# Eight experts over tokens sorted by their expert through DRAM, in place of every expert over every token

## The chip, the cores and the metric

The kernel is one program on one core of a Trainium2 chip (trn2). The metric is device time in microseconds (us), from the start of the execution to its end. A profiled execution also gives the span between its first and last recorded instruction, which is a little shorter. Engines are PE (matmuls), DVE (vector), ACT (scalar, activations), POOL (GpSimd) and SP (which here issues DMAs).

## What is computed

A network of eight stages over x, 4 batches of 512 tokens with 128 features (2048 tokens, 16 tiles of 128 rows). Each stage adds `tanh(gate) * f(layernorm(x))` to x. The stages are: a 16-head attention, **eight experts with one expert per token**, a one-head attention, a small attention with experts, a masked attention, a ternary feed-forward, a decoder block, and a mixture of 16 experts. The change is in the second stage, and reaches into the first:

```
gate_logits = einsum('bsd,ed->bse', x, gate_w) + gate_b + expert_bias
top_idx = argmax(gate_logits, axis=-1)
for e in range(8):
    mask = (top_idx == e)[..., None]
    h = relu(einsum('bsd,df->bsf', x, w1[e]) + b1[e])     # 128 -> 512
    y = einsum('bsf,fd->bsd', h, w2[e]) + b2[e]           # 512 -> 128
    out = out + mask * y
```

## The kernel before

The code is written per engine: for each stage there is one function for PE, ACT, DVE (`_ve`), POOL (`_po`) and SP, and each engine runs its functions in program order. They meet only at semaphores: `mark` names an event, `at` waits for it. Nothing reorders the instructions later. `x` stays in SBUF, token rows on partitions; `xn` is its layernorm, and `xt` is `xn` transposed (features on partitions), made by `follow_measure` (DVE, L379 to L384), `follow_power` (POOL, L389), `follow_scale` (DVE, L395), `follow_turn` (PE, L424) and `follow_turned` (ACT, L430). A batch's x of the next stage is measured as soon as it is final.

Matmuls that must be exact to fp32 are made from bf16 halves: a value is its high part plus a low part, and `products` (L449) issues three matmuls (high x high, high x low, low x high). `split_po` splits the experts' weights w1 and w2 on POOL during the first stage, so that `split_view` gives for each block of 512 columns the high and the low part.

**First stage** (`image_*`): 256 steps, one per batch, head and query tile. In a step PE makes 128x666 scores (L638), DVE takes the maximum (L692), ACT the exponential (L790), PE transposes (L649), ACT and DVE copy (L805, L710), POOL subtracts the high part to get the low part (L903), and PE multiplies with the values (L665). `image_chores(i)` says which extra work a step carries. Every eight steps SP issues two DMAs that copy keys between partition halves (`work<-work`). The last four pieces of the stage are PE's output products L593, each followed by DVE's addition to x (L739).

**Experts' stage** (`experts_*`): 32 rounds, for each batch b of 512 tokens and each expert e. `up` issues 4 x 3 matmuls of 512 columns (weights stationary, `xt1` moving) into banks 0 to 4. ACT evicts every bank twice with relu, once rounded to bf16 as the high part (L1021) and once whole (L1024), DVE subtracts them to the low part (L1043). `down` issues for 4 token tiles and 4 parts of the hidden width 3 matmuls of 128 columns, hidden activations stationary and w2 moving, so its result has token rows on partitions. DVE adds it to x with the weight `hot * gate` (L1052), which is 0 for tokens of other experts. All tokens thus go through all experts. PE's order is up(0), up(1), then the turn of batch 3, the router (L476), the one-hot and the biases b2 (L483, L989), then up(k), down(k-1) for all k. The next stage's x of batches 0 to 2 is measured, scaled and turned between the rounds. The stage begins when the last x of the first stage is added (`barrier(…, 1)`) and ends with the last L1052. `experts_sp` loads the weights of four later stages at its start.

## Time and profile before

| | us |
|---|---|
| median of 3 runs | 2153.85 |
| lowest and highest run | 2153.39, 2156.68 |
| the profiled execution's own time | 2150.68 |
| its span | 2148.9 |
| PE, DVE, ACT, POOL busy in the span | 1728.8, 1321.8, 966.7, 599.1 |
| granted PE clock, mean over the span | 0.895 |

The profile is of one execution. Its page groups busy time by engine and line, and follows back the chain of work that ended last. A granted clock of 1.00 stands for TensorE's 2.4 GHz, 0.50 for 1.2 GHz. Busy time of PE is of pipelined matmuls with modelled ends, so durations of many in a row are read from starts.

### The profile page before, as it was taken

What the parts mean: (1) busy time and instruction counts of PE and PEld (TensorE: products, weight loads), DVE (VectorE), ACT (ScalarE), POOL (GpSimd) and SP (SyncE); (2) the same over time, 40 slices, a digit from 0 to 9 for tenths busy, and PEclk for the clock granted to TensorE, in tenths of its full rate; (3) what the DMA queues carried; (4) which work ended last, traced back from release to release, by engine and by line L of the source; (5) the groups of instructions that cost most, each with busy time, mean ns of one, the idle gap of its engine ahead of it and who ended that gap; (6) DMA issues with size and microseconds to landing.
All of it is one profiled execution on the core that took longest, in us unless ns stands there. A gap on an engine that the chain in (4) does not pass through costs nothing.

```text
span 2148.9 us, 34188 instructions
## 1 busy us (share of the span) xinstructions
PE 1728.8 (80%) x12709; PEld 1075.3 (50%) x12848; DVE 1321.8 (62%) x3131; ACT 966.7 (45%) x2073; POOL 599.1 (28%) x723
## 2 busy tenths in 40 slices
PE   4899889988988987999623978996985886579997
PEld 2566656665666655776413644552444333424444
DVE  6777677767767744776487575655457455643333
ACT  4677557756766744997100633553321443201111
POOL 3567567656545540000000224200001200200000
PEclk9999989998999997999665788998997787789998
DMA  5000000000000001001000000000000000000000
GB/s 206 14 14 21 14 14 14 20 14 14 14 14 17 17 9 72 2 2 69 6 0 0 1 8 5 1 2 1 1 1 1 1 1 1 0 0 0 6 5 10
DMA packets 14598, 33.01 MB, mean 15 GB/s; under 512 B 3594, under 2 KB 9058, under 8 KB 13538
## 3 DMA queue, kind: packets, MB, share of 16 engines
q1 hardware_dynamic: 14433, 30.81, 4.6%
q8 instruction: 104, 1.70, 0.3%
q14 instruction: 61, 0.49, 0.1%
HBM read 18.84 MB, written 1.05 MB: 9 GB/s over the span
## 4 chain that ended last, share of the span: by engine, by line
PE 56%; DVE 27%; issue 7%; ACT 7%; POOL 2%; DMA 0%; ACTq 0%; DVEq 0%; POOLq 0%
PE banks L449 14%; DVE work L692 4%; PE banks L649 4%; PE banks L665 3%; PE banks L2288 3%; PE banks L1672 3%; PE banks L638 3%; PE banks L2284 3%; DVE xn L395 2%; DVE work L710 2%; ACT work L790 2%; PE banks L593 2%; PE banks L1655 1%; PE banks L424 1%; PE banks L2336 1%
## 5 line engine op out<-in xcount | busy, mean ns | idle before, releaser
L903 POOL TENSOR_TENSOR work<-work 128x512 bf16<-128x512 f32 (+1 forms) x448 | 374.1, 862 | 79.5 <-ACT work L805 75.7
L790 ACT ACTIVATE work<-banks,work 128x666 f32<-128x666 f32 x256 | 208.5, 814 | 251.3 <-DVE work L692 172.3
L649 PE MATMUL banks<-const,work 128*128 128x128 f32 (+1 forms) x1536 | 234.8, 285 | 51.1 <-ACT work L805 45.2
L389 POOL TENSOR_TENSOR norm_room<-norm_room,minus_half 128x4 f32<-128x4 f32 x48 | 50.0, 1041 | 757.1 <-DVE norm_room L384 757.1
L692 DVE TENSOR_REDUCE work<-banks 128x1 f32<-128x666 f32 x256 | 215.8, 843 | 63.7 <-PE banks L638 63.1
L649 PEld LDWEIGHTS banks<-const,work 128*128 128x128 f32 (+1 forms) x1536 | 158.3, 136 | 101.9 <-ACT work L790 53.2
L449 PE MATMUL banks<-work,weights_b 128*128 128x512 bf16 x823 | 192.6, 389 | 16.2 <-DVE work L1996 5.6
L665 PE MATMUL banks<-work 128*64 128x256 bf16 (+1 forms) x2304 | 177.7, 283 | 11.6 <-POOL work L903 10.5
L638 PE MATMUL banks<-work 128*128 128x154 bf16 (+1 forms) x980 | 182.7, 308 | 3.1 <-ACT work L790 0.4
L805 ACT ACTIVATE work<-banks 128x512 f32<-128x512 f32 x256 | 150.7, 589 | 3.3 <-PE banks L649 3.3
L424 PE MATMUL banks<-const,xn 128*128 128x128 f32 x176 | 40.2, 370 | 129.5 <-DVE xn L395 80.9
L638 PEld LDWEIGHTS banks<-work 128*128 128x128 bf16 x1024 | 97.8, 99 | 88.5 <-issue 9.9
L449 PEld LDWEIGHTS banks<-work,weights_b 128*128 128x128 bf16 x864 | 84.2, 100 | 114.9 <-issue 19.1
L1749 DVE TENSOR_REDUCE work<-banks 128x2 f32<-128x308 f32 x192 | 86.9, 473 | 79.5 <-PE banks L1627 45.3
L665 PEld LDWEIGHTS banks<-work 128*64 128x64 bf16 (+1 forms) x2304 | 108.7, 108 | 52.4 <-issue 14.8
L430 ACT ACTIVATE xt<-banks 128x512 f32<-128x512 f32 x48 | 28.7, 597 | 222.6 <-PE banks L424 222.5
L710 DVE COPY work<-banks 128x256 f32<-128x256 f32 x256 | 106.2, 415 | 32.8 <-PE banks L649 30.7
L1043 DVE TENSOR_TENSOR work<-work 128x512 bf16<-128x512 f32 x128 | 87.7, 691 | 44.2 <-ACT work L1024 42.9
L1728 ACT ACTIVATE work<-banks 128x256 f32<-128x256 f32 (+1 forms) x256 | 87.5, 382 | 59.5 <-PE banks L1659 26.9
L449 PEld LDWEIGHTS banks<-weights_b,work 128*128 128x128 bf16 x1728 | 102.9, 100 | 9.2 <-issue 1.5
L449 PE MATMUL banks<-weights_b,work 128*128 128x128 bf16 x1728 | 105.9, 223 | 1.1 <-DVE work L1043 1.1
L1021 ACT ACTIVATE work<-banks,weights_b 128x512 bf16<-128x512 f32 x128 | 90.0, 703 | 25.2 <-PE banks L449 24.8
(348 smaller groups left out, 3268.2 us busy)
## 6 DMA issues: line engine op xcount, KB each, us to landing
work<-work SPq DMA_DIRECT2D x64, 166.5 KB, 2.7
weights_b<-in_weights SPq DMA_DIRECT2D x1, 4116.0 KB, 23.1
weights_b<-in_weights SPq DMA_DIRECT2D x1, 2824.0 KB, 9.9
weights_a<-in_weights SPq DMA_DIRECT2D x1, 2056.0 KB, 10.6
weights_a<-in_weights SPq DMA_DIRECT2D x1, 2050.0 KB, 10.0
rows<-in_rows SPq DMA_DIRECT2D x1, 1496.0 KB, 13.1
weights_c<-in_weights SPq DMA_DIRECT2D x1, 1288.0 KB, 5.8
weights_b<-in_weights SPq DMA_DIRECT2D x1, 1027.5 KB, 12.0
```

The source lines that it names most:

```text
L449: m = pe.matmul(out, left(a), right(b), start=start and n == 0, stop=stop and n == 2)
L638: m = pe.matmul(slot[:, a:z], lhs, k[:, h, part, a:z], start=part == 0, stop=part == 1)
L649: m = pe.transpose(ps[0:rows, c:c + P], prob[:, t * P:t * P + rows], self.eye)
L665: m = pe.matmul(self.out_bank[64 * h:64 * h + 64, 0:2 * P], self.v[n % 3][0:rows, t, of_values, 64 * h:64 * h + 64], self.probs_parts[u % ...
L692: ve.tensor_reduce(self.neg_max[i % 4], self.slot[i % 2][:, 0:KEYS0], AX_X, ALU.max, negate=True).then_inc(self.mark("max"))
L710: ve.tensor_copy(self.probs_t[u % 2][:, h, 4:KT0, j * P:(j + 1) * P], self.bank_b[:, 0:2 * P].rearrange("p (t n) -> p t n", t=2)).then_inc ...
L790: ac.activation(self.probs[i % 4], self.slot[i % 2][:, 0:KEYS0], ACT.Exp, bias=self.neg_max[i % 4], accum_out=self.sums[u % 2][:, 2 * j + ...
L805: ac.activation(self.probs_t[u % 2][:, h, 0:4, j * P:(j + 1) * P], self.bank_a.rearrange("p (t n) -> p t n", t=4), ACT.Copy).then_inc(self ...
L903: po.tensor_tensor(parts[:, :, :, 0], exact, parts[:, :, :, 1], ALU.subtract).then_inc(self.mark(event, i - 3))
L1021: ac.activation(h[:, 0, f, :], bank, ACT.Relu, bias=col)
L1043: ve.tensor_tensor(h[:, 1, f, :], self.whole1[(FT * k + f) % 3], h[:, 0, f, :], ALU.subtract).then_inc(self.mark("hidden1", k, f))
L1728: ac.activation(out, self.bank_of(k, HALF)[0:rows_n, :], ACT.Exp).then_inc(self.mark("exp4", s, n))
```

## The change

Each token goes through its own expert alone. A DRAM tensor `sorted` has 8 regions of 2048 rows, one for each expert, and a padding of 256 rows; a row is 128 features and, as its 129th word, the token's number. `xn` gets rows of 129 words for that (`xn_rows`).

- **Routing.** `route_logits_pe`, `route_hot_ve`, `route_ranks_pe` and `route_places_ve` compute each token's row: the expert's region plus the count of earlier tokens of that expert (matmuls with a triangle and with ones). For the first 12 tiles (batches 0 to 2) this is done in the first stage, at steps 212 and 215; for the last 4 tiles at the start of the experts' stage.
- **Sends.** `route_send_po`: an indirect DMA on POOL's queue scatters a tile's 128 rows to `sorted`, 12 in steps 217 to 228 of the first stage, 4 in the experts' stage. Before, `pads_sp` fills `sorted` with rows whose number is 2048 (10 DMAs of SP, 8.6 MB in all, after the key copies of groups 2 to 11).
- **Blocks.** `route_blocks_ve` computes a table of 15 blocks of 256 rows (an expert's tokens fill whole blocks; 15 is enough for any split of 2048 tokens over 8). PE, ACT and SP each load 15 values of it into registers (`table_of`), for the weights' offset, the biases' column and the block's row.
- **Per block.** SP loads 256 rows (129 words each) into one of 7 buffers. PE transposes two tiles, ACT copies them out, DVE takes the low part in place. PE makes 12 matmuls of 256 columns (`up`), ACT evicts four times once (relu), DVE takes low parts in two operations of 512. PE makes 12 matmuls of 256 columns (`down`, now weights stationary), ACT adds b2 (one eviction), PE transposes back, DVE copies 128x256 to one of 3 buffers, and POOL scatters it with 2 indirect DMAs to the rows of `added` in DRAM; padding rows are out of bounds and are dropped. PE's order in step s is transpose(s), up(s-1), down(s-2), back(s-3).
- **End.** After all scatters SP loads `added` in four DMAs, DVE adds it to x batch by batch and measures batches 0 to 2 in between; scaling and turning these now comes after the last addition.
- Gone are the double eviction, the one-hot turned for b2 (L483, L989), and the weighted additions L1052. Some semaphores are shared under one name, and constants grow by 112 fp32 and 256 bf16 columns.

```diff
+SORT, SORTED = 256, 15
+PADS = EXPERTS * TOKENS
+PAD_PARTS, ROUTED = 10, 12
...
+        route = i - 8 * PAIRS * (BATCH - 1) - 20
+        if route in (0, 3):
+            out.append((("logits", None, None, "ranks")[route], 0))
+        elif 5 <= route < 5 + ROUTED:
+            out.append(("send", route - 5))
...
+                elif what == "send":
+                    self.route_send_po(po, b)
...
+            if 2 <= n < 2 + PAD_PARTS:
+                self.pads_sp(sp, n - 2)
...
+        self.sorted1 = [self.place(2, P + 1) for _ in range(7)]
+        self.columns1 = [self.place(SORT) for _ in range(2)]
+        self.hidden1 = [self.place(FT, SORT) for _ in range(2)]
+        self.back1 = [self.place(2, P) for _ in range(3)]
+        self.added1 = self.place(TILES, P)
...
+    def route_logits_pe(self, pe, part, k):
...
+        for n, t in enumerate(tiles):
+            m = pe.matmul(bank[:, n * EXPERTS:(n + 1) * EXPERTS], self.xt[:, t * P:(t + 1) * P], self.w[1]["gate"], start=True, stop=True)
+        m.then_inc(self.mark("routed", 1, part))
+    def route_ranks_pe(self, pe, part, k):
...
+        m = pe.matmul(bank[:, 0:n * EXPERTS], before, flat(tiles.start, tiles.stop), start=True, stop=False, skip_group_check=True)
+        for back in range(1, n):
+            m = pe.matmul(bank[:, back * EXPERTS:n * EXPERTS], ones, flat(tiles.start, tiles.stop - back), start=False, stop=False,
...
+    def route_places_ve(self, ve, part, k):
...
+        ve.tensor_copy(self.place1[:, tiles], self.number1[:, 0:n]).then_inc(self.mark("places1", part))
...
+    def route_send_po(self, po, t):
...
+        po.indirect_dma_start(self.dram["sorted"], bass.IndirectOffsetOnAxis(ap=self.place1[:, t:t + 1], axis=0),
+                              self.xn_rows[:, t, :], None).then_inc(self.mark("dma_sent", n=16), 16)
+    def pads_sp(self, sp, part):
...
+        src = self.dram["pads"].unsqueeze(0).to_broadcast([rows // P, P, P + 1])
+        sp.dma_start(out, src).then_inc(self.mark("dma_pads", n=16), 16)
...
+    def route_blocks_ve(self, ve, k):
...
+        ve.tensor_scalar(self.table1[:, 0, :], self.row1[one], float(PADS // SORT), float(SORT), ALU.min, ALU.mult)
+        ve.tensor_scalar(self.table1[:, 1, :], self.expert1[one], float(e - 1), float(2 * FF), ALU.min, ALU.mult)
+        ve.tensor_scalar(self.table1[:, 2, :], self.expert1[one], float(e - 1), None, ALU.min).then_inc(self.mark("placed1", 1))
...
+    def table_of(self, eng, n, name, top):
+        eng.wait_ge(*self.at("placed1", 1))
+        registers = [eng.alloc_register(f"{name}{s}") for s in range(SORTED)]
+        eng.reg_load(registers, self.table1[0:1, n, 0:SORTED])
+        return [eng.snap(r, min_val=0, max_val=top) for r in registers]
     def experts_pe(self, pe):
         self.barrier(pe, 1)
+        self.follow_turn(pe, 0, BATCH - 1)
+        self.route_logits_pe(pe, 1, 6)
+        self.route_ranks_pe(pe, 1, 6)
...
+        expert = self.table_of(pe, 1, "pe_expert", (EXPERTS - 1) * 2 * FF)
...
+        def weights(name, s, f, part):
+            at = part * FF + f * P
+            return self.w[1][name].bitcast(BF16)[:, at:at + span][:, bass.ds(expert[s], P)]
+
+        def up(s):
+            pe.wait_ge(*self.at("columns1_low", s))
+            x = self.halves(self.columns1[s % 2])
             for f in range(FT):
+                if f % 2 == 0:
+                    bank = self.bank(pe, 2 + 2 * (s % 2) + f // 2, "relu1", s, f + 1)
+                self.products(pe, bank[:, f % 2 * SORT:(f % 2 + 1) * SORT], lambda part: weights("w1", s, f, part),
+                              lambda part: x[:, :, 1 - part], True, True).then_inc(self.mark("up1", s, f))
...
+        def down(s):
+            bank = self.bank(pe, 6, "shifted1", s)
+            for f in range(FT):
+                if f % 2 == 0:
+                    pe.wait_ge(*self.at("relu1_low", s, f // 2))
+                h = self.halves(self.hidden1[s % 2][:, f, :])
+                m = self.products(pe, bank[:, 0:SORT], lambda part: weights("w2", s, f, part), lambda part: h[:, :, 1 - part], f == 0, f == FT - 1)
+            m.then_inc(self.mark("weighed1", s))
...
+        def back(s):
+            pe.wait_ge(*self.at("shifted1", s))
+            bank = self.bank(pe, 7, "back1", s)
+            for h in (0, 1):
+                m = pe.transpose(bank[:, h * P:(h + 1) * P], self.down1[s % 2][:, h * P:(h + 1) * P], self.eye)
...
+        for s in range(SORTED + 3):
+            if s < SORTED:
+                for h in (0, 1):
+                    m = pe.transpose(bank[:, h * P:(h + 1) * P], self.sorted1[s % 7][:, h, 0:P], self.eye)
...
+            if 0 <= s - 1 < SORTED:
+                up(s - 1)
+            if 0 <= s - 2 < SORTED:
+                down(s - 2)
+            if s >= 3:
+                back(s - 3)
+        for b in range(BATCH - 1):
+            self.follow_turn(pe, 1, b)
     def experts_ac(self, ac):
...
+        self.follow_turned(ac, 0, BATCH - 1)
+        expert = self.table_of(ac, 2, "ac_expert", EXPERTS - 1)
+        for s in range(SORTED + 2):
+            if s < SORTED:
+                if s >= 2:
+                    ac.wait_ge(*self.at("up1", s - 2, FT - 1))
+                ac.activation(self.columns1[s % 2], self.bank_of(s % 2, SORT), ACT.Copy).then_inc(self.mark("columns1", s))
...
+            if 0 <= s - 1 < SORTED:
+                o = s - 1
+                for f in range(FT):
...
+                    col = w["b1"][:, f * EXPERTS:(f + 1) * EXPERTS][:, bass.ds(expert[o], 1)]
+                    ac.activation(self.hidden1[o % 2][:, f, :], src, ACT.Relu, bias=col).then_inc(self.mark("relu1", o, f))
+            if s >= 2:
+                ac.wait_ge(*self.at("weighed1", o))
...
+                ac.activation(self.down1[o % 2], self.bank_of(6, SORT), ACT.Identity, bias=w["b2"][:, bass.ds(expert[o], 1)]).then_inc(self.mark("shifted1", o))
+        for b in range(BATCH - 1):
+            self.follow_turned(ac, 1, b)
...
     def experts_ve(self, ve):
...
+        self.route_hot_ve(ve, 1, 6)
+        self.route_places_ve(ve, 1, 6)
+        self.route_blocks_ve(ve, 6)
+        for s in range(SORTED + 3):
+            if s < SORTED:
...
+                ve.tensor_tensor(x[:, :, 0], self.columns1[s % 2], x[:, :, 1], ALU.subtract).then_inc(self.mark("columns1_low", s))
+            if 0 <= s - 1 < SORTED:
+                o = s - 1
+                for g in (0, 1):
...
+                    ve.tensor_tensor(h[:, :, 0], whole, h[:, :, 1], ALU.subtract).then_inc(self.mark("relu1_low", o, g))
+            if s >= 3:
+                o = s - 3
...
+                if o >= 3:
+                    ve.wait_ge(*self.at(f"dma_back{o % 3}", 32 * (o // 3)))
+                ve.tensor_copy(self.back1[o % 3], self.bank_of(7, SORT).rearrange("p (h d) -> p h d", h=2)).then_inc(self.mark("back1", o))
+        for b in range(BATCH):
+            ve.wait_ge(*self.at(f"dma_x{b}", 32))
+            rows = self.rows_of(b)
+            ve.scalar_tensor_tensor(self.x[:, rows, :], self.added1[:, rows, :], self.gates[:, 4:5], self.x[:, rows, :], ALU.mult,
+                                    ALU.add).then_inc(self.mark("x1", b))
+            if b < BATCH - 1:
+                self.follow_measure(ve, 1, b)
+        for b in range(BATCH - 1):
+            self.follow_scale(ve, 1, b)
     def experts_po(self, po):
         self.follow_power(po, 0, BATCH - 1)
+        for t in range(ROUTED, TILES):
+            self.route_send_po(po, t)
+        for s in range(SORTED):
+            po.wait_ge(*self.at("back1", s))
...
+                token = self.sorted1[s % 7][:, h, P:P + 1].bitcast(I32)
+                po.indirect_dma_start(self.dram["added"], bass.IndirectOffsetOnAxis(ap=token, axis=0), self.back1[s % 3][:, h, :],
+                                      None, bounds_check=TOKENS - 1, oob_is_err=False).then_inc(self.mark(f"dma_back{s % 3}", n=16), 16)
...
     def experts_sp(self, sp):
         self.barrier(sp, 1)
...
+        row = self.table_of(sp, 0, "sp_row", PADS)
+        sp.wait_ge(*self.at("dma_sent", 16 * TILES))
+        for s in range(SORTED):
+            if s >= 3:
+                sp.wait_ge(*self.at("sorted1", s - 3))
+            if s >= 7:
...
+            src = self.dram["sorted"][bass.ds(row[s], SORT), :].rearrange("(h p) w -> p h w", p=P)
+            sp.dma_start(self.sorted1[s % 7], src).then_inc(self.mark(f"dma_sorted{s % 3}", n=16), 16)
...
+        for k in range(3):
+            sp.wait_ge(*self.at(f"dma_back{k}", 32 * len(range(k, SORTED, 3))))
+        src = self.dram["added"].rearrange("(t p) d -> p t d", p=P)
+        for b in range(BATCH):
+            rows = self.rows_of(b)
+            sp.dma_start(self.added1[:, rows, :], src[:, rows, :]).then_inc(self.mark(f"dma_x{b}", n=16), 16)
```

**PE, the experts' stage before**, from the first rounds on (a row is consecutive instructions of one line; weights_b holds w1 and w2, work the activations):

```order
L449 MATMUL banks<-work,weights_b 128x512 x24
L424 MATMUL banks<-const,xn 128x128 x4
L476 MATMUL banks<-weights_b,xt 128x8 x16
L483 MATMUL banks<-const,work 8x128 x16
L989 MATMUL banks<-small,work 128x128 x16
L449 MATMUL banks<-weights_b,work 128x128 x48
L449 MATMUL banks<-work,weights_b 128x512 x12
```

The rounds of 12 matmuls of 512 columns and 48 of 128 columns repeat 31 times. **PE after the change**, from the end of step 3 into step 4 (L1161 is `back`, L1169 the transposes of a block, L475 `products`; ISA is an instruction on registers, here the address of weights):

```order
L1161 MATMUL banks<-const,work 128x128 x2
L1169 MATMUL banks<-const,work 128x128 x2
L475 ISA
L475 MATMUL banks<-work,weights_b 128x256 x2
L475 ISA
L475 MATMUL banks<-work,weights_b 128x256
L475 ISA
```

Before every use of another weight tile stands a register instruction; a full block has 24 matmuls of 256 columns, 16 such instructions and 4 transposes.

**POOL in the first stage, before** (`image_po`; L884 spreads the sums' inverses, L903 subtracts high parts):

```order
L903 TENSOR_TENSOR work<-work 128x4x128
L884 COPY work<-work 128x256
L903 TENSOR_TENSOR work<-work 128x4x128
L903 TENSOR_TENSOR work<-work 128x2x128
L903 TENSOR_TENSOR work<-work 128x4x128
L903 TENSOR_TENSOR work<-work 128x2x128
```

One step's subtractions follow the other's. **After the change, steps 216 to 218** (L926 and L947 are the same two lines, `sorted<-xn,places` is a send):

```order
L947 TENSOR_TENSOR work<-work 128x4x128
L926 COPY work<-work 128x256
L947 TENSOR_TENSOR work<-work 128x4x128
L947 TENSOR_TENSOR work<-work 128x2x128
L1081 DMA sorted<-xn,places 16640x129
L947 TENSOR_TENSOR work<-work 128x4x128
L947 TENSOR_TENSOR work<-work 128x2x128
L1081 DMA sorted<-xn,places 16640x129
```

From step 217 to step 228 a send stands before each step's subtractions.

**SP in the experts' stage before** (from the last key copies on):

```order
L934 DMA work<-work 64x1332 x64
L352 DMA weights_c<-in_weights 128x386
L352 DMA weights_c<-in_weights 128x2576
L352 DMA weights_c<-in_weights 128x515
L352 DMA weights_a<-in_weights 128x4112
L352 DMA weights_b<-in_weights 128x5648
L352 DMA weights_b<-in_weights 128x2055
```

It held only the loads of later weights. **After the change**, the first load of a block, and the last rows of the stage (L1123 and L1124 load the table into registers):

```order
L1123 TENSOR_LOAD table
L1124 ISA x2
L1270 ISA
L1270 DMA work<-sorted 128x2x129
L378 DMA weights_a<-in_weights 128x4112
L1277 DMA work<-added 128x4x128 x4
L378 DMA weights_b<-in_weights 128x5648
```

Each of the 15 block loads has a register instruction before it, and the four loads of `added` are the stage's last. On PE the turns of batches 0 to 2 (L424), before in rounds 11, 19 and 27, now stand behind the last `back`, and the next stage's first matmuls, before directly behind the barrier, stand behind them.

## Rows read from the trace of the kernel before

**Rows 1.** The page of the kernel before, its parts 1 and 4.
```profile
PE 1728.8 (80%) x12709; PEld 1075.3 (50%) x12848; DVE 1321.8 (62%) x3131; ACT 966.7 (45%) x2073; POOL 599.1 (28%) x723
...
PE 56%; DVE 27%; issue 7%; ACT 7%; POOL 2%; DMA 0%; ACTq 0%; DVEq 0%; POOLq 0%
```

**Rows 2.** The windows view; per engine busy us (instructions), then granted clock, DMA share, GB/s.
```profile
650.00:720.00 70.00, 62.12 (x566) 42.63 (x571) 50.92 (x107) 46.36 (x107) 39.45 (x51) 0.98 0.06 15
804.50:841.20 36.70, 21.85 (x108) 16.31 (x110) 14.30 (x43) 12.94 (x22) 1.01 (x1) 0.68 0.27 107
841.20:1010.60 169.40, 165.45 (x1880) 124.21 (x1909) 124.78 (x294) 145.46 (x246) 4.14 (x3) 0.99 0.01 2
1010.60:1030.00 19.40, 14.10 (x71) 9.07 (x71) 8.59 (x30) 6.61 (x22) 1.01 (x1) 0.99 0.51 204
1030.00:1076.00 46.00, 29.68 (x105) 22.12 (x105) 21.79 (x83) 6.06 (x21) 3.02 (x3) 0.57 0.00 0
```

**Rows 3.** The chain that ended last: start us, us, what; the experts' stage and its end.
```profile
920.24 5.22 PE banks L449 x59
925.51 5.22 PE banks L449 x59
...
1009.42 1.14 DVE x L1052 x4
1010.60 1.31 PE banks L1141 x8
```

**Rows 4.** Groups by form, 804.5 to 1010.6 us: xcount | busy us, mean ns | idle before us.
```profile
L449 PE MATMUL banks<-weights_b,work 128*128 128x128 bf16 x1536 | 92.9, 221 | 1.1 <-DVE work L1043 1.1
L1024 ACT ACTIVATE work<-banks,weights_b 128x512 f32<-128x512 f32 x128 | 90.6, 708 | 0.0
...
L1043 DVE TENSOR_TENSOR work<-work 128x512 bf16<-128x512 f32 x128 | 87.7, 691 | 44.2 <-ACT work L1024 42.9
L449 PE MATMUL banks<-work,weights_b 128*128 128x512 bf16 x353 | 81.2, 379 | 3.9 <-DVE work L1006 2.3
...
L389 POOL TENSOR_TENSOR norm_room<-norm_room,minus_half 128x4 f32<-128x4 f32 x4 | 5.1, 1286 | 181.9 <-DVE norm_room L384 181.9
```

**Rows 5.** The timeline, 802 to 832 us: start us, us, engine line op, what it waited for.
```profile
802.10 2.02 PE L593 MATMUL banks<-weights_a,work 128*128 128x128 f32 x16 [0.54 <-DVE x L739]
...
817.08 0.87 DVE L379 BATCH_NORM_STATS2 norm_room<-x 128x6 f32<-128x128 f32 x4
...
820.86 1.12 PE L424 MATMUL banks<-const,xn 128*128 128x128 f32 x4 [9.29 <-DVE xn L395]
822.01 0.60 ACT L430 ACTIVATE xt<-banks 128x512 f32<-128x512 f32 x1 [5.57 <-PE banks L424]
...
822.75 6.97 PE L476 MATMUL banks<-weights_b,xt 128*128 128x8 f32 x32 [0.78 <-ACT xt L430]
...
830.74 0.29 DVE L467 TENSOR_TENSOR work<-work 128x128 f32<-128x128 f32 x1
```

**Rows 6.** Groups by form in the first stage, 650 to 720 us.
```profile
L903 POOL TENSOR_TENSOR work<-work 128x512 bf16<-128x512 f32 x25 | 26.1, 1045 | 10.0 <-ACT work L805 9.8
...
L903 POOL TENSOR_TENSOR work<-work 128x256 bf16<-128x256 f32 x19 | 11.7, 617 | 0.0
L710 DVE COPY work<-banks 128x256 f32<-128x256 f32 x24 | 9.9, 413 | 1.8 <-PE banks L649 1.6
...
L884 POOL COPY work<-work 128x256 f32<-128x256 f32 x6 | 2.4, 398 | 15.7 <-DVE work L700 15.7
L799 ACT ACTIVATE work<-banks 128x256 f32<-128x256 f32 x6 | 2.2, 374 | 0.0
```

**Rows 7.** The DMA view: issues, KB each, median us to landing.
```profile
work<-work SPq DMA_DIRECT2D x64, 166.5 KB, 2.7
...
x<-in_x SPq DMA_DIRECT2D x4, 256.0 KB, 3.9
```

**Rows 8.** POOL's smallest operation, by its line: duration ns min/median/max.
```profile
L389 POOL TENSOR_TENSOR norm_room<-norm_room,minus_half x48: 1007/1009/1381, 265.3 to 1863.8; 128x4 f32<-128x4 f32 x48
```

294 lines of the change are left out of this document (156 added, 138 removed).

## The prediction

> **What bounds the kernel now.** I read the page first. PE is busy 80% of the span, and the chain that ended last runs 56% through PE and 27% through DVE [rows 1], so work taken from PE can count. The windows then separate the stages. The experts' stage starts after PE's last product of the first stage and the addition behind it, at 804.5 us [rows 5], and ends with the last L1052 at 1009.42 + 1.14 = 1010.6 us [rows 3]: 206.1 us. From 841.2 on PE is busy 165.45 of 169.40 us at clock 0.99, ACT 145, DVE 125, and POOL 4 [rows 2]. The chain there is PE alone, one round each 925.51 - 920.24 = 5.27 us [rows 3]; ACT waits for PE little and DVE waits for ACT [rows 4]. So the stage is bound by PE's columns: 32 rounds of 5.27 are 169 us. The other 37 us are its start: two rounds, then the routing, in which PE stands at a mean clock of 0.68 [rows 2].
>
> **What is removed.** A round holds 12 x 512 + 48 x 128 = 12288 columns in 5.27 us, 0.429 ns each, which is the 2.4 GHz level. A block of the change holds 24 x 256 = 6144. 32 rounds become 15 blocks, a fixed number whatever the routing, so 393 thousand columns become 92 thousand: 169 us become 40. ACT's 256 evictions of about 0.7 us [rows 4] and DVE's 128 subtractions of 0.69 go too.
>
> **A block's period.** Four engines work on consecutive blocks, so the period is the longest of these:
> - PE: 6144 x 0.429 = 2.64 us, and 4 transposes of 128x128 fp32 at 2.02 / 16 = 0.126 [rows 5], 0.5; together 3.15. The 16 register instructions have no row. Below they cost 0, if the queue runs ahead of the array. Above, the slowest pace of narrow PE work in the trace, 6.97 / 32 = 0.218 us [rows 5], gives 3.5. In a round a 128-column matmul with its weight load takes 55 ns; I take that, as the next weight load needs the address: 0.9. PE 4.05 us (3.15 to 6.65).
> - ACT: 6 evictions of 256 columns at 0.374 [rows 6]: 2.25.
> - DVE: two low parts of 512 at 0.69 [rows 4], one of 256 and one copy at 0.41 each [rows 6]: 2.2.
> - POOL: two scatters, for which the trace has nothing like. Call c the time one holds POOL. Below, its smallest operation takes 1.01 us [rows 8]. Above, a copy of 166 KB by SP's queue lands in 2.7 us [rows 7], if POOL is held until then. I take the middle, 1.9, not the lower end, since POOL's small operation took 1.29 on the mean beside the experts' DVE work against 1.01 elsewhere [rows 4, 8], and the same kind of DVE work stands in each block. POOL 3.8 us (2.0 to 5.4).
> - SP: a load of 132 KB lands in about 2.7 us with three in flight: 0.9.
>
> So the period is 4.05 us, with PE and POOL nearly level. Between `up` and the `down` that needs it stand four relus and a subtraction, 4 x 0.374 + 0.7 = 2.2 us plus handovers, against `down`, `back`, two transposes and `up` of other blocks, about 3.2 us: covered, with under a microsecond to spare.
>
> **The stage's sum.**
> 1. Measuring to transposed batch 3: as from 817.08 to 822.61 now, 5.5 us [rows 5]. Logits of 4 tiles, a quarter of 6.97: 1.7. Eleven narrow DVE operations at 0.25 (a 128-wide one takes 0.29 [rows 5]): 2.8. Thirteen narrow matmuls at half of 0.218: 1.4. Sum 11.4.
> 2. Four sends 4c = 7.6, and 2.7 to land: 10.3. Behind them hide the 13 DVE operations of the table (3.3) and the register loads, which are free up to 7 us; if the sends shrink to 4.0 + 2.7, up to 3.4 us.
> 3. The first block's load: 2.7.
> 4. 15 x 4.05 = 60.8; 3 for the pipeline's ends; 3 because PE comes from idling, and the L424 transposes after such a gap take 1.12 us for four [rows 5], twice the warm 0.126 each: 66.8.
> 5. The end, all exposed: copy 0.4, two scatters 3.8, landing 2.7, reading `added` 3.9 as the loads of x [rows 7], four additions of 0.69 with three measurings of 1.5 between: 7.3. Sum 18.1.
> 6. The next stage starts later than its barrier: three scalings of about 1.1 (the stretch 817.08 to 820.86 holds measuring, POOL's 1.0 and one scaling) are now in front, and PE is cold for its first matmuls, where before it was at 0.99 to 1030 us [rows 2]: 3.3 + 2.7 = 6.
>
> Together 115.3 us in place of 206.1: **-90.8 us**.
>
> **The first stage** pays for what is moved there. POOL is busy 39.45 of 70 us [rows 2] in 25 steps (25 subtractions of 512 [rows 6]), so it has 1.2 us free in a step of 2.8. A send of 1.9 overfills each of twelve steps by 0.7, 8.4 us in all; PE waits for POOL's subtractions only once per four steps, so I count 7. The routing of 12 tiles adds 13 DVE operations (3.9 us) and some 3 us on PE, which is busy 62 of 70: 3 more. The 10 fills of 0.86 MB share SP's queue with the key copies, but eight steps (22 us) separate those; a load of x, 256 KB, lands in 3.9, so a fill ends within 13: nothing. Together **+10 us** (2 to 26).
>
> Net -80.8. The profiled execution took 2150.68, so the same would take 2069.9; the median of the runs shown is 3.2 higher, which gives **2073 us**.
>
> On the scatter's cost a page speaks for a better result. The Trainium skill, "DMA: Bandwidth & Descriptors", section "Anatomy of one DMA — SWDGE (gpsimd) path", puts a DMA of this queue at about 2.0 us plus bytes / 436e3, most of it waiting for the write receipt. A 64 KB scatter would by that land in 2.15 us and hold POOL for much less, and the sum would be that of the first rival. No run here shows a DMA issued by POOL.
>
> **Rivals.**
> - *Cheap scatters* (0.21). c = 1.0 and register instructions hidden: the period is PE's 3.15. Against my sum that is 15 x 0.9 = 13.5, 3.6 in the sends, 1.8 at the end and 7 in the first stage: 26 less, 2047 us. For it: in its rounds PE issues two instructions per 55 ns with no loss. Against it: it needs both unknowns at their low ends.
> - *PE bound by addresses, or at half clock* (0.16). At 0.218 per register instruction the period is 6.65; at 1.2 GHz it would be 6.3. 15 x 2.6 = 39 more: 2112 us. For it: from 1030 to 1076 PE was busy 29.7 of 46 us and the clock 0.57 [rows 2]. Against it: at 14.1 busy of 19.4 it was 0.99, and PE's share of a block is above that. The Trainium skill, "TensorE: Matmul & The Clock Gate", section "Why this matters for your kernels", asks for no long idle gaps between bursts; by it the blocks, whose gaps are under 1 us, stay at full clock.
> - *The first stage hides nothing* (0.09). All twelve sends hold up the chain: 12 x 1.9 = 23 in place of 7: 2089 us.
> - *Slower: scatters bound by their rows* (0.07). If POOL works through a scatter's 128 rows one by one, c can be far above 2.7. Both scatters of a block, four sends, two at the end and twelve in the first stage count: 15 x (2c - 4.05) + 18 x (c - 1.9), which uses up the whole gain at c = 3.7, 29 ns per row. At c = 4.5: 121 more, 2194 us. For it: the operation is software with a data-dependent address per row, and there is no row to exclude it. The Trainium skill, "GPSIMD Engine Reference", section "Performance pitfalls for Q7 kernels", gives about 102 cycles for each small read command, as one per index; 128 of them at the 1.2 GHz of its specifications would be an estimated 10.9 us, and the time about 2500. No row bears that out.
>
> **How the numbers follow.** The forecast has 0.44 (its own range 2055 to 2095), the rivals 0.53, and 0.03 is left for what I do not see. Within 0.2% (4 us), about what a measurement of this kernel can tell from no change, hardly any case ends: 0.01. Faster is forecast, cheap scatters, PE bound, first stage, and part of the slow one's low side: 0.90; slower 0.09. The range takes in the first rival below and the second above, with 5 and 10 us for their other terms: 2042 to 2122.
>
> **What would show it.** In the profile after: PE's block period near 4 us at a clock above 0.9, the experts' stage near 115 us, a POOL queue with sends about 1.9 us apart, 2 us between the last scatter and the loads of `added`, and steps 217 to 228 longer by about 0.6 us each. The forecast is wrong if blocks take over 5.5 us, or if the scatters in a row stand over 3 us apart; then the wait before `back`'s copy on DVE names POOL. If the routing at the start takes over 30 us, items 1 and 2 were mis-sized.

## The result, and the profile after

| | before | after |
|---|---|---|
| median, us | 2153.62 (4 runs, 2144.13 to 2156.68) | 2049.88 (4 runs, 2045.83 to 2055.41) |
| the profiled execution | 2150.68, span 2148.9 | 2045.83, span 2044.0 |

The ratio is 0.9527 with a 95% interval of 0.9489 to 0.9565: about 102 us faster, where 80.8 were forecast. Five more runs of the changed kernel, beside other experiments, lay at 2047.76 to 2057.56, so the median of all nine is 2052.3. All lie in the forecast range of 2042 to 2122, near its lower end.

The page of the changed kernel, its parts 1 and 4, against [rows 1]:

```profile
PE 1609.7 (79%) x11325; PEld 984.1 (48%) x11325; DVE 1233.4 (60%) x2948; ACT 845.6 (41%) x1899; POOL 647.0 (32%) x770
...
PE 53%; DVE 28%; issue 8%; ACT 7%; POOL 3%; DMA 1%; ACTq 0%; another core or an unknown queue 0%; DVEq 0%; POOLq 0%; SPq 0%
```

The windows view after (columns as in [rows 2]), one row for each part of the forecast's sum:

```profile
650.00:720.00 70.00, 63.90 (x566) 43.98 (x565) 47.56 (x102) 44.73 (x103) 47.82 (x59) 0.94 0.10 27
802.83:822.55 19.72, 3.45 (x25) 2.92 (x26) 7.12 (x37) 0.60 (x1) 4.97 (x5) 0.56 0.34 116
822.55:829.00 6.45, 6.09 (x27) 3.92 (x28) 2.60 (x5) 2.86 (x8) 0.00 (x0) 0.50 0.29 76
829.00:859.00 30.00, 30.00 (x261) 25.52 (x260) 20.42 (x36) 20.88 (x54) 16.03 (x15) 1.00 0.21 56
859.00:881.00 22.00, 16.38 (x136) 12.97 (x134) 10.68 (x20) 11.51 (x29) 12.23 (x12) 1.00 0.37 129
881.00:897.60 16.60, 0.00 (x0) 0.00 (x0) 7.35 (x33) 0.00 (x0) 7.46 (x7) 0.59 0.23 63
897.60:916.30 18.70, 13.55 (x48) 8.28 (x48) 8.31 (x33) 4.80 (x8) 1.83 (x2) 0.73 0.52 211
```

The experts' stage runs from 802.83 to 897.55 us: 94.7 us in place of 206.1. PE's steady part is the fourth row: busy all of its 30 us at clock 1.00, POOL 16.03. In the third row PE is busy 6.09 of 6.45 us as well, but at the 1.2 GHz level, behind the 20 us of routing in which it did 3.45 us of work. The chain of waits in the steady part, start us, us, what:

```profile
834.12 0.22 PE banks L1161 x2
834.34 0.22 PE banks L1169 x2
834.55 2.79 PE banks L475 x24
837.34 0.22 PE banks L1161 x2
```

A block takes 837.34 - 834.12 = 3.22 us: two transposes back (L1161), two of the next tiles (L1169) at 0.11 each, and 24 matmuls in 2.79. Before, the rounds of 5.27 us of [rows 3] stood in its place. The groups by form, 829 to 859 us (columns as in [rows 4]):

```profile
L475 PE MATMUL banks<-work,weights_b 128*128 128x256 bf16 x227 | 28.2, 279 | 0.0
...
L1253 POOL DMA_INDIRECT added<-work x15 | 16.6, 1104 | 24.2 <-DVE work L1234 18.1 <-issue 6.1
```

L475 (the blocks' matmuls) has no idle time ahead of it, with 16 register instructions in each block. L1253, the scatter, is the operation that no row of before had: most of POOL's idle time before it is put down to DVE's copy (L1234), so POOL waits for work and does not hold it up. The timeline after, of the stage's start, its end, and the handover (columns as in [rows 5]):

```profile
806.79 1.09 PE L450 MATMUL banks<-const,xn 128*128 128x128 f32 x4 [4.36 <-DVE xn L421]
808.63 1.87 PE L1018 MATMUL banks<-weights_b,xt 128*128 128x8 f32 x8 [0.75 <-ACT xt L456]
813.52 0.17 DVE L1068 CAST places<-scratch 128x4 int32<-128x4 f32 x1
813.98 1.05 POOL L1081 DMA_INDIRECT sorted<-xn,places  x1 [8.43 <-DVE places L1068]
815.33 0.96 POOL L1081 DMA_INDIRECT sorted<-xn,places  x1 [0.30 <-issue]
...
820.33 11.53 SPq L1270 DMA_DIRECT2D work<-sorted  x7
822.55 1.50 PE L1169 MATMUL banks<-const,work 128*128 128x128 f32 x4 [9.74 <-DMA work<-sorted]
...
880.90 0.42 DVE L1234 COPY work<-banks 128x256 f32<-128x256 f32 x1 [0.59 <-issue]
885.05 0.98 POOL L1253 DMA_INDIRECT added<-work  x1 [0.30 <-issue]
887.23 2.03 SPq L1277 DMA_DIRECT2D work<-added  x4
890.27 0.75 DVE L1238 SCALAR_TENSOR_TENSOR x<-work,gates,x 128x512 f32<-128x512 f32 x1 [8.94 <-DMA work<-added]
896.81 0.74 DVE L1238 SCALAR_TENSOR_TENSOR x<-work,gates,x 128x512 f32<-128x512 f32 x1
897.47 3.16 DVE L421 TENSOR_SCALAR xn<-x,norm_room 128x128 f32<-128x128 f32 x12
...
902.39 1.09 PE L450 MATMUL banks<-const,xn 128*128 128x128 f32 x4 [0.78 <-ACT xt L456]
903.27 2.26 PE L1317 MATMUL banks<-context,weights_c 128*128 128x154 f32 x8
```

The sends and scatters shown here (L1081, L1253) hold POOL for 0.96 to 1.05 us, and the next one starts 0.30 us after the end of the one before: starts are 1.26 to 1.35 us apart. Over all 30 scatters the median is 0.98 us and the longest 1.45; in the blocks, beside DVE's work, the mean is 1.10. In the handover the next stage's first matmuls (L1317) take 2.26 us for what took 1.31 in [rows 3], behind three turns that were not in their way before.

| part of the sum | forecast | this profile |
|---|---|---|
| 1 measuring to the places of batch 3 | 11.4 | 10.9 (802.83 to 813.69) |
| 2 four sends and landing | 10.3 | 6.6 (to 820.33) |
| 3 first block's load | 2.7 | 2.2 (to 822.55) |
| 4 blocks, with their ends | 66.8 | 58.3 (to 880.90) |
| 5 end | 18.1 | 16.7 (to 897.55) |
| 6 handover, more than before | 6 | 7.8 |
| first stage | +10 | -1.7 |

The handover is read from the last addition's end to the next stage's first scores: 1010.56 to 1021.55, 11.0 us, before and 897.55 to 916.33, 18.8, after. From there to the end of the span it is 1127.4 us before and 1127.7 after. The sum of the parts is 94.7 - 206.1 + 7.8 + 0.3 - 1.7 = -105.0, the difference of the spans to 0.1.

The first stage was to lose 10 us and won 1.7. Its step starts, read from DVE's maximum of each step, show two things. Ahead of the routing the change is 8.9 us early: step 211 starts at 659.94 against 668.86, and 3.25 of these 8.9 us are there when step 0 starts (32.60 against 35.85). Steps 211 to 218 take 25.3 us against 18.0, and from step 218 on (the sends) nothing is lost: steps 218 to 228 take 27.04 against 27.07. What the routing does, in the timeline of the change:

```profile
663.97 3.98 PE L1018 MATMUL banks<-weights_b,xt 128*128 128x8 f32 x24 [0.72 <-DVE work L745]
...
669.03 1.29 PE L673 MATMUL banks<-work 128*128 128x512 bf16 x4
```

The logits of 12 tiles hold PE for 3.98 us (0.166 for each of the 24 matmuls, and PE's weight loads are busy for 3.91 of it), and four score matmuls (L673, two of 512 and two of 154 columns) behind them take 1.29 us where they take 0.73 elsewhere. The clock had gone to its lower level: the granted clock is 1.00 from 660 to 664 us, 0.85 and 0.50 in the two halves of the logits' 4 us, and 0.50 in the 1.29 us of the scores.

### The profile page after: what moved, and what is told of

Same layout as the page of the kernel before. It is cut to its first block, busy times and chain, and to the rows that moved or that the text cites. A ratio compares the mean times of both kernels' runs of the same rounds, so it can differ in the third digit from the quotient of the medians.

```text
span 2044.0 us, 31410 instructions
## 1 busy us (share of the span) xinstructions
PE 1609.7 (79%) x11325; PEld 984.1 (48%) x11325; DVE 1233.4 (60%) x2948; ACT 845.6 (41%) x1899; POOL 647.0 (32%) x770
## 4 chain that ended last, share of the span: by engine, by line
PE 53%; DVE 28%; issue 8%; ACT 7%; POOL 3%; DMA 1%; ACTq 0%; another core or an unknown queue 0%; DVEq 0%; POOLq 0%; SPq 0%
PE banks L475 9%; DVE work L727 5%; PE banks L684 4%; PE banks L700 3%; PE banks L2465 3%; PE banks L1849 3%; PE banks L673 3%; PE banks L2461 3%; DVE xn L421 3%; DVE work L745 2%; PE banks L450 2%; ACT work L829 2%; PE banks L628 2%; PE banks L1832 2%; PE banks L2513 1%
## 5 line engine op out<-in xcount | busy, mean ns | idle before, releaser
L947 POOL TENSOR_TENSOR work<-work 128x512 bf16<-128x512 f32 (+1 forms) x448 | 373.7, 861 | 76.8 <-ACT work L844 73.2
L415 POOL TENSOR_TENSOR norm_room<-norm_room,minus_half 128x4 f32<-128x4 f32 x48 | 50.1, 1045 | 573.2 <-DVE norm_room L410 573.2
L673 PE MATMUL banks<-work 128*128 128x512 bf16 (+1 forms) x1024 | 190.5, 309 | 0.4 <-issue 0.3
L475 PE MATMUL banks<-work,weights_b 128*128 128x512 bf16 (+1 forms) x840 | 161.6, 352 | 15.5 <-ACT work L1206 4.9
L673 PEld LDWEIGHTS banks<-work 128*128 128x128 bf16 x1024 | 97.1, 99 | 86.6 <-issue 7.4
L475 PEld LDWEIGHTS banks<-work,weights_b 128*128 128x128 bf16 (+1 forms) x840 | 83.5, 101 | 89.1 <-issue 25.3
L450 PEld LDWEIGHTS banks<-const,xn 128*128 128x128 f32 x176 | 27.1, 189 | 155.2 <-DVE xn L421 72.4
L739 DVE TENSOR_TENSOR work<-banks,work 128x256 f32<-128x256 f32 x64 | 27.2, 424 | 85.6 <-ACT work L838 85.6
L926 POOL COPY work<-work 128x256 f32<-128x256 f32 x64 | 25.4, 397 | 167.1 <-DVE work L735 167.1
L1832 PE MATMUL banks<-work 128*128 128x256 bf16 (+1 forms) x256 | 65.9, 289 | 14.2 <-ACT work L1897 11.6
```

The lines of the kernel that those rows point to most:

```text
L450: i = pe.transpose(ps[:, j * P:j * P + rows], src[0:rows, j, :], self.eye[0:rows, 0:rows])
L475: m = pe.matmul(out, left(a), right(b), start=start and n == 0, stop=stop and n == 2)
L673: m = pe.matmul(slot[:, a:z], lhs, k[:, h, part, a:z], start=part == 0, stop=part == 1)
L947: po.tensor_tensor(parts[:, :, :, 0], exact, parts[:, :, :, 1], ALU.subtract).then_inc(self.mark(event, i - 3))
L1832: m = pe.matmul(bank, left, a.q4[b % 2][:, g, cols], start=True, stop=s != 4)
```

## Experiments

Twelve runs, each with the changed kernel as its base. Because the times of one kernel scatter by some 10 us, the table gives stretches of each profile, in us. The columns are:

- *step 211*: when it starts;
- *211-218*: from that start to the start of step 218;
- *to blocks*: from the first stage's last addition to the first transposes of a block;
- *blocks and landing*: from these transposes to the first addition of `added`;
- *to scores*: from that addition to the next stage's first scores;
- *rest*: from these scores to the end of the span.

A *long period* is a block, among those of 3.22 us, that takes 3.5 us or more.

| profile | step 211 | 211-218 | to blocks | blocks and landing | to scores | rest |
|---|---|---|---|---|---|---|
| before | 668.9 | 18.0 | | | | 1127.4 |
| change | 659.9 | 25.3 | 20.1 | 67.7 | 26.1 | 1127.7 |
| change again | 667.9 | 25.3 | 20.3 | 61.8 | 25.7 | 1137.4 |
| fixed weights | 663.9 | 25.3 | 20.5 | 63.7 | 26.2 | 1131.1 |
| twelve blocks | 667.5 | 25.3 | 20.2 | 58.0 | 25.9 | 1134.2 |
| extra scatters | 660.5 | 25.3 | 20.1 | 110.3 | 25.2 | 1126.8 |
| extra scatters again | 668.2 | 25.3 | 20.1 | 95.0 | 26.2 | 1131.1 |
| extra, fixed weights | 667.3 | 25.3 | 20.4 | 94.3 | 26.4 | 1134.7 |
| logits split | 663.5 | 28.8 | 20.3 | 67.8 | 25.8 | 1134.0 |
| late routing | 663.7 | 18.0 | 20.2 | 62.9 | 26.4 | 1131.3 |
| one logit tile | 668.5 | 21.7 | 20.1 | 65.0 | 25.9 | 1130.8 |
| late load | 663.9 | 25.3 | 20.3 | 63.0 | 26.3 | 1135.0 |
| handover order | 664.0 | 25.3 | 20.1 | 63.0 | 23.8 | 1130.7 |
| handover and scale | 662.9 | 25.3 | 20.2 | 63.2 | 21.8 | 1136.3 |

**Fixed weights.** Do the 16 register instructions of a block cost PE anything?

```diff
-            return self.w[1][name].bitcast(BF16)[:, at:at + span][:, bass.ds(expert[s], P)]
+            return self.w[1][name].bitcast(BF16)[:, at + (s // 2) * 2 * FF:at + (s // 2) * 2 * FF + P]
```

> Edit: PE's weights of block s lie at a fixed offset, those of expert s // 2, so the 16 register instructions of each block are gone from PE; everything else stays (the output is then that of other experts' weights). Theory A (PE's queue runs ahead of the array, as in the change's profile, where a steady block takes 3.23 us): the block stays at 3.2 us, the time within 2 us of the change's 2050. Theory B (an instruction still costs a little, hidden in other slack, or makes the late blocks slip): the steady block falls towards 3.15 or the 5.5 us of slips near the end vanish, 3 to 7 us faster. My forecast's 0.9 us per block would give 13.5 us, and a block of 2.3, which PE's columns alone exclude.

Measured: 2052.6 us (2 runs). The steady period, from the timeline:

```profile
844.53 0.38 PE L1161 MATMUL banks<-const,work 128*128 128x128 f32 x2
...
847.76 0.38 PE L1161 MATMUL banks<-const,work 128*128 128x128 f32 x2
```

It is 3.23 us again. PE's register instructions cost a block nothing, and my 0.9 us for them is refuted. This profile has no long periods among its blocks, where the change's has two of 4.8 and 4.6 us; whether that is the edit's doing is open here, and the section's end comes back to it.

**Twelve blocks.** Counted with the reference and these inputs, the experts have 368, 214, 357, 259, 365, 234, 81 and 170 tokens, which fill 12 blocks; three of 15 hold only padding. The edit runs 12 (`BLOCKS = 12` in all loops over blocks). It would be wrong for an uneven split, so it is a measurement and no version.

> Edit: 12 blocks are run in place of 15 (the three left out hold only padding with these inputs, so nothing is missing). If the period of 3.23 us is all that a block costs: 9.7 us faster than the change. If the slips seen at the end (two periods of 4.6 to 4.8 us) come from the last blocks of the count, they move with the end and the gain is 9.7; if they come at a fixed place or time, one may drop out and the gain is 11 to 13. Below 8: the end of the stage is bound by the scatters in POOL's queue and not by PE.

Measured: 2050.23 us (4 runs, 2039.21 to 2053.82), not separable from the change by its times. In the table its blocks take 58.0 us against 67.7: 9.7 less for three blocks, as 3 x 3.23 would give. That equality is partly luck, since both profiles hold some long periods (3.9 to 5.2 us in this one), and how much they add differs from profile to profile; against profiles without any, 63, this one is 5 us shorter. So what a block costs is read from the steady periods and not from this difference.

**Extra scatters.** Is POOL near being the bound, and does a scatter's time follow its rows?

```diff
-                po.indirect_dma_start(self.dram["added"], ...
+                for to, r in (("spare_added", slice(0, 64)), ("added", slice(0, P))):
+                    token = self.sorted1[s % 7][r, h, P:P + 1].bitcast(I32)
+                    po.indirect_dma_start(self.dram[to], ..., self.back1[s % 3][r, h, :], ...
```

> Edit: ahead of each of the 30 scatters of 128 rows stands one of 64 rows to a spare tensor. Theory A (an indirect DMA holds POOL for a fixed time whatever its rows, 0.98 us and 0.30 to the next): POOL needs 4 x 1.28 = 5.1 us a block, becomes the bound, and the stage grows by about 15 x 1.9 = 28 us, more at its end; the 64-row scatter is as long as the 128-row one. Theory C (time follows the rows): the short one takes 0.5, a block's POOL 3.6 to 3.8, and the stage grows by 6 to 9 us. Theory D (with slack, POOL is no bound and what counts is the landing): within 3 us.

Measured: 2094.75 us (2 runs, 2087.42 and 2102.09). The groups by form on POOL, 834 to 880 us:

```profile
L1254 POOL DMA_INDIRECT added<-work x14 | 14.2, 1018 | 4.3 <-issue 4.3
L1254 POOL DMA_INDIRECT spare_added<-work x14 | 13.4, 955 | 27.4 <-DVE work L1234 24.0 <-issue 3.3
```

Half the rows are 6% shorter, so time does not follow rows (theory C falls). By the medians of the two kinds, 0.91 and 0.98, a block's four scatters stand 4 x 0.30 + 2 x 0.91 + 2 x 0.98 = 4.98 us. But the stretch of the blocks grew by 42.5 us, more than 15 x 1.75 = 26, and PE shows single matmuls with gaps:

```profile
843.20 0.28 PE L475 MATMUL banks<-work,weights_b 128*128 128x256 bf16 x1 [0.46 <-issue]
...
844.61 0.27 PE L475 MATMUL banks<-work,weights_b 128*128 128x256 bf16 x1 [1.13 <-issue]
```

**Extra scatters with fixed weights**, to see whether those gaps are PE's register instructions held up:

> Edit: the extra scatter of 64 rows ahead of each of the 30 and, with it, PE's weights at fixed offsets as in the fixed-weights run (output of other experts' weights). With the extra scatters alone the stage grew by 42.5 us, more than POOL's 15 x 1.9, and PE's matmuls stood singly with 0.5 to 1.8 us between them. Theory A (register instructions of PE are held up while the scatters are written): now the periods are POOL's 4 x 1.25 = 5.0 us, evenly, and the stage is 13 to 18 us shorter than with the extra scatters alone. Theory B (it is the loads of blocks or anything else that the scatters delay): the single matmuls and the 42 us stay.

Measured: 2086.15 us (2 runs), the stretch 94.3, no single matmuls, and, from the fifth on, periods of 5.1 to 5.5 us with one of 8.1 and some of 3.2 to 4.2. That looked like theory A. The same kernel as in the first run of extra scatters decides:

> Edit: none against the run with extra scatters of 64 rows. There single matmuls stood 0.5 to 1.8 us apart and the stretch from the first transposes to the first addition was 110.3 us; with fixed weights beside it 94.3. Theory A (the gaps come and go between executions): this time 92 to 98 us. Theory B (register instructions on PE are held up by the scatters): 105 to 115 us again, with gaps between single matmuls.

Measured: 2083.06 us (2 runs), and 95.0 us with register instructions in place. So register instructions alone do not make the gaps of the first run; that run was on another chip, so the gaps may be its execution's or its chip's. What is left is the cost of a POOL that is the bound: 94.3 and 95.0 against 61.8 to 63.7 in the profiles without long periods, 31 to 33 us. The periods account for 26 of them, and no row was read for the other 5 to 7.

**Logits split.** Would smaller pieces of the routing cost the first stage less?

```diff
-        if route in (0, 3):
-            out.append((("logits", None, None, "ranks")[route], 0))
+        if route in (0, 1, 2):
+            out.append(("logits", route))
+        elif route == 4:
+            out.append(("ranks", 0))
```

Each piece makes 4 tiles' logits, and DVE adds the gate's bias to them at once, which frees the bank.

> Edit: the logits of the first 12 tiles are made 4 tiles a step at steps 212, 213 and 214 with one DVE operation each, ranks one step later and sends one step later. The change's routing put the chain of the first stage back by 7.9 us within five steps: 24 matmuls of 8 columns took 3.98 us of PE in one piece, and the granted clock fell behind them. Theory E (the piece is as long as its weight loads, and PE has no room): 1.3 us in each of three steps, the setback stays 6 to 8 us. Theory F (half of it is the clock and the waiting for the one piece): the setback falls to 3 to 5 us, the time 3 to 5 us lower.

Measured: 2060.95 us (4 runs), some 8 slower than the change. Steps 211 to 218 take 28.8 us, 10.8 over before and 3.5 over the change; the other 5 us of the 8 are not in these steps, and this profile has long periods. Every piece has its wait of 0.68 to 1.63 us in front. Behind the first and the third the clock is at 0.50, behind the second, as long as the first, the scores run at full clock; here the first two pieces and the scores after them:

```profile
667.55 1.03 PE L1024 MATMUL banks<-weights_b,xt 128*128 128x8 f32 x8 [0.72 <-DVE work L747]
...
669.33 1.29 PE L675 MATMUL banks<-work 128*128 128x512 bf16 x4
...
673.66 1.03 PE L1024 MATMUL banks<-weights_b,xt 128*128 128x8 f32 x8 [0.68 <-DVE work L747]
674.54 0.73 PE L675 MATMUL banks<-work 128*128 128x512 bf16 x4
```

Both theories fall: a part of the cost is paid once for each piece, the wait each time and the half clock in two of three.

**Late routing.** `route = i - 8 * PAIRS * (BATCH - 1) - 60` in place of `- 20`.

> Edit: the routing of the first 12 tiles and its 12 sends stand 40 steps later: logits at step 252, ranks at 255, sends at steps 257 to 268, where the first stage runs out and PE and POOL have less to do. In the change steps 211 to 218 take 25.3 us where they took 18.0. Theory A (the cost of the routing is PE's time and clock in full steps): most of the 7.3 us go, and the sends, 12 x 1.28 = 15.4 us, fit before the last addition, 4 to 7 us won. Theory B (at the end the chain is as tight, and the sends put back the start of the experts' stage): what the steps win is lost between step 255 and the first block, within 2 us of the change.

Measured: 2054.09 us (4 runs). Steps 211 to 218 take 17.95 us, as before the change: the 7.3 us are the routing's. But its last addition comes at 810.2 with step 211 at 663.7, 146.5 us, where the change needs 142.5. Theory B, and 4 us worse: steps 228 to 255 take 75.8 us where they took 69.5, so the routing costs 6.4 there too, and from step 255 to the last addition it is 25.7 in place of 20.8. POOL's rows there show sends of about 1 us between the last subtractions, where the steps run out and POOL has no idle time left to hold them; that these sends are the 4.9 us is argued from the rows, and no run leaves them out:

```profile
791.29 1.62 POOL L947 TENSOR_TENSOR work<-work 128x512 bf16<-128x512 f32 x2
793.08 0.98 POOL L1081 DMA_INDIRECT sorted<-xn,places  x1 [0.17 <-issue]
794.10 1.61 POOL L947 TENSOR_TENSOR work<-work 128x512 bf16<-128x512 f32 x2
```

**One logit tile.** In `route_logits_pe`, part 0, all but the first tile are skipped.

> Edit: of the logits of 12 tiles in the first stage only the first tile's are made (2 of 24 matmuls of 8 columns); the other 11 tiles are routed by what stood in the bank, so their tokens go to arbitrary experts. DVE's operations, ranks and sends stay. Steps 211 to 218 took 25.3 us in all profiles of the change and 18.0 before it. Theory A (the 3.98 us of narrow matmuls and the half clock behind them are the cost): 18.5 to 20 us. Theory B (DVE's 13 operations and the wait for the bank that they free): 22 to 24 us.

Measured: 2054.2 us (2 runs). Steps 211 to 218 take 21.7 us, 3.7 over before in place of 7.3. The scores behind the short piece run at full clock, and the next maximum waits behind the routing's narrow operations on DVE, which start at 673.04; ACT waits for it:

```profile
672.54 0.36 PE L1020 MATMUL banks<-weights_b,xt 128*128 128x8 f32 x2 [0.72 <-DVE work L745]
...
673.49 0.74 PE L673 MATMUL banks<-work 128*128 128x512 bf16 x4
...
676.20 0.84 DVE L727 TENSOR_REDUCE work<-banks 128x1 f32<-128x666 f32 x1
677.13 0.82 ACT L829 ACTIVATE work<-banks,work 128x666 f32<-128x666 f32 x1 [2.47 <-DVE work L727]
```

So the long piece and the half clock behind it are one half of the cost, 3.6 us. Of the other half the step starts put 2.4 us at the steps with the logits (212 to 214) and 1.3 at the steps with the ranks (215 and 216), where the change has 6.0 and 1.3. The rows above name DVE's narrow operations for the 2.4; the ranks' part has its own matmuls and operations, and no run takes them apart. Each theory had half.

**Late load.** SP's load of weights_a (2 MB) behind the loads of `added`.

> Edit: SP issues the 2 MB load of weights_a behind the loads of `added`, not ahead of them. The change's profile has two periods of 4.8 and 4.6 us among blocks of 3.23, the second right behind that load's issue. Theory A (the load's packets hold up the scatters or PE's instructions): the period of 4.6 goes, the stage is 1.5 to 4 us shorter from first transposes to the first addition (67.7 us in the change). Theory B (it has nothing to do with it): 67 to 68 us; the fixed-weights run, in which no period was long while this load stood in its place, speaks for B.

Measured: 2051.13 us (2 runs), 63.0 us, no long periods. Alone it would speak for theory A. Handover order and late routing, with that load in its old place and on the same chip, have 63.0 and 62.9 and no long periods either, so it does not.

**Handover order.** The waits behind the barrier, where the experts' stage hands over to the next one, are the one loss that looked avoidable.

```diff
             self.x ... ALU.add).then_inc(self.mark("x1", b))
+            if b > 1:
+                self.follow_scale(ve, 1, b - 2)
             if b < BATCH - 1:
                 self.follow_measure(ve, 1, b)
-        for b in range(BATCH - 1):
-            self.follow_scale(ve, 1, b)
+        self.follow_scale(ve, 1, BATCH - 2)
```

On PE and ACT the turn of batch 2 stands behind the next stage's keys.

> Edit: DVE scales batch 0 behind the addition of batch 2 and batch 1 behind that of batch 3; PE and ACT turn batches 0 and 1 in the experts' stage, make the next stage's keys, and turn batch 2 behind them. In the change's profile 18.8 us lie between the last addition and the first weighing of the next stage, 11.0 before the change. Theory A (the order of the turns and scalings behind the barrier makes the handover longer): the 18.8 fall to 13 to 15, the last addition comes 1 us later, 3 to 4 us won. Theory B (PE's half clock after 10 us of idling makes it): 18 stay. The times scatter by some 8 us, so the stretch in the profile decides.

Measured: 2049.41 us (4 runs). From the last addition's end to the scores:

```profile
907.21 1.11 DVE L421 TENSOR_SCALAR xn<-x,norm_room 128x128 f32<-128x128 f32 x4
908.37 0.66 PE L450 MATMUL banks<-const,xn 128*128 128x128 f32 x4 [1.87 <-DVE xn L421]
...
913.57 2.36 PE L1339 MATMUL banks<-work 128*128 128x154 f32 x16
```

913.57 - 897.93 = 15.6 us in place of 18.8; from the first addition's start to the last one's it takes 7.4 in place of 6.5. Net 2.3 us against the change's first profile, less than the 3 to 4 expected. Batch 3's scaling at 907.21 stands behind an eviction on DVE, and PE waits 1.87 us for it.

**Handover and scale.** That scaling is moved ahead of the evictions too.

> Edit: the handover order, and batch 3's scaling ahead of the two evictions of the next stage's queries on DVE, so that its turn on PE does not wait for them. The handover order took the stretch from the last addition to the next stage's scores from 18.8 to 15.6 us, at 0.9 more before the last addition. Theory A (PE then waited 1.9 us for batch 3's scaled rows): the stretch falls to about 13.7, 4 us below the change over both stretches, so the median is some 4 us below that of the change run beside it. Theory B (the chain goes through the evictions on DVE): 15 to 16 us, 2 us below.

```profile
901.55 1.11 DVE L421 TENSOR_SCALAR xn<-x,norm_room 128x128 f32<-128x128 f32 x4 [1.12 <-POOL norm_room L415]
...
910.61 2.36 PE L1339 MATMUL banks<-work 128*128 128x154 f32 x16
```

From 896.98 to 910.61 it is 13.6 us, and from the first addition to the scores 21.8, against 25.2 to 26.4 in the eleven profiles that keep the old handover: 3.4 to 4.6 won there. The median is 2049.11 (5 runs, 2048.72 to 2054.51) against 2052.68 (2047.76 to 2057.56) for the change, measured together with it. The ranges overlap, and the ratios to before are the same, 0.9536 each. The gain is shown in the profile and not in the times.

**The change again**, for what is the kernel's and what the execution's:

> Edit: none, the changed kernel once more. In seven profiles the steady period is 3.22 to 3.23 us; long periods (3.4 to 5 us) stand in four with register instructions (the change, twelve blocks, logits split, extra scatters) and in none of three others with them (handover, late load, late routing), nor in fixed weights. Theory A (long periods come and go between executions of the same kernel): no tie to an edit; this profile has either none, with 63 us from the first transposes to the first addition, or some, with 65 to 68. Theory B (they belong to this kernel's instructions): two periods of 4.6 to 4.8 us as in the first profile. The end of the first stage comes at 802.5, 806.5 or 810 us, as step 0 starts at 32.6 or 35.8.

Measured: the profiled execution has a span of 2055.7 us, 11.7 over the first one, without any long period. Theory A, with one reservation below. The table shows where profiles differ in stretches whose code is equal: step 211 starts at 660 to 668.5; the blocks take 62 to 64 or 65 to 68; the rest takes 1127 to 1137. The first profile of the change happened to be early at step 211 and short in the rest, and late in its blocks.

What a long period consists of can be read, in the change's first profile:

```profile
859.61 0.84 ACT L1200 ACTIVATE work<-banks,weights_b 128x256 f32<-128x256 f32 x2 [1.95 <-PE banks L475]
861.83 0.84 ACT L1200 ACTIVATE work<-banks,weights_b 128x256 f32<-128x256 f32 x2 [1.39 <-PE banks L475]
...
863.17 1.57 PE L475 MATMUL banks<-work,weights_b 128*128 128x256 bf16 x12 [1.42 <-ACT work L1206]
```

The four relus (L1200) belong to a block whose matmuls start at 856.98. In steady blocks they start 1.0 to 1.3 us behind the first of these matmuls and follow each other without a gap; here they start 2.6 us behind it and stand in two pairs with 1.4 us between, though PE's `up` had ended by 858.5. ACT's eviction L1206 comes late by that, and PE waits for it between `up` and `down`. The same wait, before the second 12 matmuls of a block, stands in the long periods of all four profiles that have them. So ACT is what runs late. ACT too forms addresses in registers, for its bias columns, and no run takes these away; and the record names the chip for each experiment: two chips gave five profiles with plain scatters and no long period among them, two others gave four, three of which have long periods. Neither was varied alone.

## Why the prediction was right or wrong

**What bounds, and what is removed: right.** The rounds' 169 us went, and the blocks are bound by PE's columns: 24 matmuls in 2.79 us, against the 2.64 that the rounds' 0.429 ns a column gave. But the signs that were to show the forecast did not appear: blocks take 3.22 us and not near 4, the stage 94.7 and not 115, sends stand 1.26 to 1.35 us apart and not 1.9, and steps 218 to 228 are no longer than before.

**The period, item 4: wrong, twice on the same side.** "PE 4.05 us": the 16 register instructions cost nothing and the period is 3.22 us, which fixed weights leave at 3.23. "POOL 3.8 us (2.0 to 5.4)": a scatter costs 1.28, a block 2.6, and POOL is busy 16.03 of 30 us. I had placed c in the middle, at 1.9, since POOL's small operation was slow beside the experts' DVE work. That row was of another kind of operation: the scatter takes 0.98 us at the median and 1.10 on the mean beside the new DVE work, with 1.45 at most. The lower bound, 1.01 from POOL's smallest operation, was close to the value; with the 0.30 between two, which the forecast had no term for, it is 1.28. So in the blocks the rival "cheap scatters" happened, with its 3.15 for PE. The extra scatters then show that its opposite is real: at 4.98 us on POOL a block follows POOL. The rule of the slower rival, 15 x (POOL's time for a block - the period), gives 26 of the 31 to 33 us that this costs.

**Ends of the blocks.** Items 4 and 3 together took 60.5 us here for 69.5 forecast. With 12 steady periods of 3.23 and no long ones, 822.55 to 880.90 would be about 53.5 (826.72 to 880.2 in the handover order's profile), so some 5 of the 58.3 are the long periods of this profile.

**Sends, item 2**: 6.6 for 10.3, all of it c: 3 x 1.27 + 0.96 us to the end of the last, 1.5 to SP's issue. **Start and end, items 1 and 5**: 10.9 for 11.4 and 16.7 for 18.1, right within their terms. The operations for the table of blocks hid behind the sends, as said. **Handover, item 6**: right in mechanism, 7.8 for 6.

**First stage: near in the sum, wrong in both terms.** The forecast was 7 for sends and 3 for routing. The twelve sends cost nothing: c fits the 1.2 us that POOL has free. The routing costs 7.3: from step 211 to the last addition it is 142.5 us against 135.3. The step that failed is "some 3 us on PE, which is busy 62 of 70: 3 more". The 3.98 us of logits are 1 above its 3; it missed PE's wait of 0.72 us in front, the clock that falls to 0.50 within them and behind them, and the chain through DVE, whose narrow operations stand before the next maximum. The ten fills of `sorted` show no cost: from step 0 to step 211 the profiles with them take 627.3 to 635.2 us, and the one before took 633.0.

**The sum, by code alone.** 94.7 - 206.1 + 7.8 + 7.2 = -96.4 us; the other 8.6 of the 105.0 between the two profiles are 8.9 us ahead of step 211, less 0.3 in the rest, and these stretches differ as much between profiles of equal code. The 94.7 still hold the 5 us of long periods. The forecast's -80.8 was 16 us short: blocks 8.5, sends 3.7, first stage 2.8, end 1.4, start and first load 1.0, less 1.8 in the handover. The range held the time because it had been drawn down to the first rival; the forecast's own 2073 was 23 us off, with all of the large errors on one side.

**The rivals.** Cheap scatters gave 2047, and the measured time is nearer to it than to my 2073; both unknowns were at their low ends together, which I had called the case against it. Its landing so close to 2049.88 is partly luck: it had the routing at 3 us for 7.3 and no long periods, and the two profiles compared lie 8.6 us apart elsewhere. PE bound at half clock did not happen: 829 to 881 us ran at clock 1.00. Only the first 6.5 us of blocks ran at the 1.2 GHz level, for which the forecast had 3 us. The Trainium skill, "TensorE: Matmul & The Clock Gate", section "Why this matters for your kernels", asks for no long idle gaps between bursts. In the change's blocks the trace agrees, with gaps of at most 2.28 us and clock 1.00. Two other rows do not: in twelve blocks the clock is 0.50 behind a gap of the same 2.28 us (the 12 matmuls after it take 2.74 us in place of 1.57), and in the first stage it fell to 0.50 within the logits, with no gap over 0.72 us in the 8 us ahead of them. Slower by scatters bound by rows did not happen: 64 rows take 0.955 us and 128 take 1.018, and nothing like the estimate of 10.9 us for 128 rows was seen. The Trainium skill, "DMA: Bandwidth & Descriptors", section "Anatomy of one DMA — SWDGE (gpsimd) path", gives an estimated 2.15 us for a 64 KB scatter to land. The DMA view of the handover order's profile, 826 to 890 us, has 2.5:

```profile
added<-work POOLq DMA_INDIRECT x30, 2.5
```

**Open.** What makes the long periods (3.6 to 5.2 us, two to five in a profile) is not settled. They stand in the change's first profile, twelve blocks, logits split and one logit tile, and not in six others, the change itself among them, so the place of the load and PE's register instructions are excluded as a sufficient cause. That fixed weights prevent them is not shown by one profile. ACT's evictions are what comes late in them; ACT's own register instructions and the chip are rivals that no run tested. Why profiles differ by 8 us ahead of step 211 (some 3 of them before step 0) and by 10 in the rest wasn't tried.

## What to carry to other kernels

An operation without a row should be taken at the nearest bound that shares its kind of work (here an engine's smallest operation, since an indirect DMA is only issued there), and not at the middle; a run with it doubled then shows how far the engine is from being the bound. Work put into a stream that keeps an engine 90% busy is priced per piece as well as per instruction: a wait ahead, the weight loads, narrow operations that stand before another engine's work, and sometimes a lower clock behind. Where executions of equal code differ by 10 us, compare stretches between fixed points of several profiles, from the same chip where there is one, before a difference is put down to an edit; twice one profile told a story here that the same kernel's next profile took back.

## What the runs showed of the hardware

- An indirect DMA of 128 rows of 512 or 516 bytes holds POOL for 0.96 to 1.05 us in most cases (median 0.98, up to 1.45), one of 64 rows for 0.91 at the median, and 0.30 us pass before the next. It lands 2.5 us after its issue at the median (handover order).
- Register instructions that form weight addresses, 16 among 24 matmuls of 256 columns, leave PE's period unchanged (3.22 us with them, 3.23 without).
- After 20 us with 3.45 us of work PE ran at 1.2 GHz for its first 6.5 us, though busy for 6.09 of them, and at 2.4 GHz from there. After 3.98 us of matmuls with 8 columns in a stream of full clock the next four score matmuls (two of 512 and two of 154 columns) took 1.29 us in place of 0.73; after 0.36 us of the same they took 0.74. After pieces of 1.03 us it was 1.29 once and 0.73 once, so the length of the piece does not decide it alone.
- POOL's small operation (L415) takes 1.44 to 1.47 us beside DVE's additions and statistics at the stage's end; its median over the 48 of the change's profile is 1.007.
- Late relus on ACT, 1.4 us apart though PE's matmuls for them had ended, made PE wait 1.42 us and a block 4.81 us long in place of 3.22.
